# Graph attention layer: smaller halves of work, a ring of 16 tiles and rows that go through memory

## The reference, cut to what matters

```
Wh = x1 @ W;  s_i = Wh @ a1;  s_j = Wh @ a2
e = leaky_relu(s_i[:, :, None] + s_j[:, None, :], 0.2)
e = where(adj > 0 or diagonal, e, -inf)
h = softmax(e, axis=-1) @ Wh
out = layernorm(x1 + elu(h))
```

## Time and profile before

| | us |
|---|---|
| median of 3 runs | 3981.21 |
| lowest, highest | 3978.74, 4451.86 |
| the profiled execution's own time | 3980.02 |
| its span | 3978.2 |

### The profile page before, as it was taken

The page is one execution under the profiler, slowest core; times in us unless marked ns, Lnnn a source line. Parts: engine busy times, 40 slices in busy tenths (PEclk is TensorE's granted clock), DMA queues, the critical chain, the costliest instruction groups (busy, mean ns, idle before and its releaser), DMA issues. The chain is left out here.

```text
span 3978.2 us, 135900 instructions
## 1 busy us (share of the span) xinstructions
PE 3643.7 (92%) x57428; PEld 2511.2 (63%) x57428; DVE 3254.2 (82%) x3989; ACT 2520.5 (63%) x3554; POOL 2064.1 (52%) x1068
## 2 busy tenths in 40 slices
PE   6999999999999999999999999942998998999898
PEld 2656756655756655665665675522776777777777
DVE  6786887787788688688788778857989989889897
ACT  3666666666666666666666666622677676776777
POOL 1786787777678687678677768831101011011010
PEclk9999999999999999999999999976999999999999
DMA  6010010010010001001001000042111110110101
GB/s 216 3 37 16 14 40 14 19 35 19 14 40 14 14 19 40 14 14 40 18 15 35 19 14 19 19 164 78 39 43 33 44 54 24 52 54 22 33 28 37
DMA packets 106692, 145.28 MB, mean 37 GB/s; under 512 B 3792, under 2 KB 87632, under 8 KB 104016
## 3 DMA queue, kind: packets, MB, share of 16 engines
q1 hardware_dynamic: 104816, 135.80, 10.2%
q10 hardware_dynamic: 1248, 0.40, 0.1%
HBM read 102.63 MB, written 33.55 MB: 34 GB/s over the span
## 5 line engine op out<-in xcount | busy, mean ns | idle before, releaser
L277 POOL TENSOR_TENSOR psums<-probs 128x1024 f32<-128x1024 f32 x512 | 1288.8, 2517 | 626.7 <-ACT probs L381 624.4
L381 ACT ACTIVATE probs<-probs 128x1024 f32<-128x1024 f32 x1024 | 1083.5, 1058 | 812.8 <-DVE probs L857 791.2
L493 PE MATMUL ctx_ps<-probs,v_rows 64*32 64x512 f32 x16256 | 1477.1, 590 | 11.7 <-DVE seg_ctx L780 10.3
L857 DVE SCALAR_TENSOR_TENSOR probs<-sc_ps,clip_hi 128x1024 f32<-128x1024 f32 x1024 | 1225.0, 1216 | 217.6 <-PE sc_ps L480 206.6
L480 PE MATMUL sc_ps<-q_cols,k_cols 64*32 64x512 f32 x16384 | 1205.0, 592 | 43.9 <-DVE probs L857 43.3
L1324 PE MATMUL out_ps<-wh,e 128*128 128x257 f32 x4096 | 963.7, 388 | 166.0 <-DVE e L1466 157.2
L1324 PEld LDWEIGHTS out_ps<-wh,e 128*128 128x128 f32 x4096 | 777.5, 193 | 326.6 <-DVE e L1466 117.9
L493 PEld LDWEIGHTS ctx_ps<-probs,v_rows 64*32 64x32 f32 x16256 | 664.0, 106 | 289.9 <-issue 190.6
L480 PEld LDWEIGHTS sc_ps<-q_cols,k_cols 64*32 64x32 f32 x16384 | 533.8, 106 | 333.9 <-issue 212.2
L1153 POOL TENSOR_TENSOR rstd<-var_eps,minus_half 128x4 f32<-128x4 f32 x32 | 68.4, 2138 | 1069.6 <-DVE var_eps L1426 1069.6
L487 PE MATMUL den_ps<-psums,ones 64*32 64x512 f32 x4064 | 598.3, 594 | 17.9 <-DVE seg_ctx L780 11.2
(11 more groups left out here) (97 smaller groups left out, 3356.1 us busy)
## 6 DMA issues: line engine op xcount, KB each, us to landing
x_cols<-in_xT SPq DMA_DIRECT2D x8, 2048.0 KB, 7.9
probs<-in_adjT SPq DMA_DIRECT2D x16, 1024.0 KB, 8.4
x_rows<-in_x SPq DMA_DIRECT2D x32, 512.0 KB, 4.1
x<-res SPq DMA_DIRECT2D x32, 512.0 KB, 2.9
x_in<-x SPq DMA_DIRECT2D x8, 2048.0 KB, 10.3
x_res<-x SPq DMA_DIRECT2D x32, 512.0 KB, 4.7
out<-h SPq DMA_DIRECT2D x32, 512.0 KB, 3.2
e<-in_adjT SPq DMA_DIRECT2D x8, 1024.0 KB, 7.8
```

Of the source, the lines that this page charges most:

```text
L277: pool.tensor_tensor(psums[:, q % 2, pair, :], probs[:, (SJ * q) % RING, pair, :], probs[:, (SJ * q + 1) % RING, pair, :], ALU.add).then_i ...
L381: act.activation(probs[:, n % RING, pair, :], probs[:, n % RING, pair, :], ACT.Exp, scale=DH ** -0.5).then_inc(s_exp, 1)
L493: return pe.matmul(ctx_ps[quad(h), z, :], v_rows[head_rows(r), n % JB, at:at + QUAD], probs[head_rows(r), n % RING, h, :], start=start, st ...
L857: dve.scalar_tensor_tensor(out=probs[:, n % RING, pair, :], in0=sc_ps[:, p, :, :], scalar=-LIM, in1=clip_hi[:, j, c * CW:(c + 1) * CW][:, ...
```

## The change

Only `layer1` changes, save the constant BIG = 2^126.

- Mask: one DVE instruction a piece in place of two; values 0 or -BIG; the diagonal is set to 0. Maxima use add and max, masking is min(mask + BIG, e).
- Maxima by halves of 1024 queries: 32 instructions of 128 x 1024 a batch. Those of half 0 stand at steps 10 to 40 of the batch before, those of half 1 at steps 42 to 72, which is up to step 8 of the batch itself. POOL reduces twice: half 0 at chunk 3 of the batch before, half 1 at chunk 0 of the batch, ahead of that chunk's `inverse_deviation`.
- s_i is a column more of the product with W (258 columns), no longer a row made by PE. SP stores it (2048 values of 4 bytes, `spread_own`) and loads it as 128 x 16; the maxima come as 128 x 8 from partition 0. `row_operations` is four instructions of 128 x 8 for each half (steps 55 and 17). SP stores the result and loads two rows of 1024 queries to all partitions (512 KB each, `make_rows`).
- ERING 16, LRING 8, AHEAD 6, larger side two steps ahead, LATE 5, and EARLY 4: the last 4 steps of a chunk do their right tiles first, with a semaphore `s_right` of their own for `invert`, which waits for the left products before its third reciprocal.
- ELU plus one: `scale_h` adds 1, one ACT pass exp(h - 1), DVE takes max(min(exp, 1), h).
- x1 comes in pieces of 512 KB; the units of preparation are interleaved over steps 1 to 31.
- Moved: invert and scale_h and exp_h to j = 3, residual 8, stats and variance together 9, offset 11, norm_h 12.

```diff
-    ERING = 8
-    AHEAD = 3
-    LRING = 4
+    ERING = 16
+    AHEAD = 6
+    LARGER_AHEAD = 2
+    LRING = 8
-    LATE = 3
+    LATE = 5
+    EARLY = 4
+    INV_AT, ELU_AT, RES_AT, STATS_AT, OFFSET_AT = 3, 6, 8, 9, 11
+    SCALE_AT, EXP_AT, NORM_AT = 3, 3, 12
+    MAX_AT = (10, 42)
+    ROWS_AT = (55, 17)
+    FIFTHS_AT = 45
+    uses_at = [1 + 32 * u // USES for u in range(USES)]
...
+    max_at = {(0, j): MAX_AT[0] + 32 * j // JB for j in range(JB)}
+    max_at.update({(1, j): MAX_AT[1] + 32 * j // JB for j in range(JB)})
...
+            def spread_own(b):
+                sp.wait_ge(s_prepread, count(b, USES, 2 + USES))
+                    sp.dma_start(s_d[0].rearrange("(j p) -> p j", p=P), wh[:, b[1] % 2, :, 0]).then_inc(s_sout, 16)
+                sp.wait_ge(s_sout, count(b, 16, 16))
+                sp.wait_ge(s_rows, count(b, 8))
+                sp.dma_start(s_c[:, :, :], s_d[0].rearrange("(h p j) -> p h j", h=2, p=P)).then_inc(s_sin, 16)
+            def make_rows(b, half, first=False):
+                sp.wait_ge(s_all, count(b, 2, 2 + half + 1))
+                sp.dma_start(m_c[:, :], highest[0:1, :].rearrange("o (q j) -> o q j", j=HJ)).then_inc(s_m, 16)
+                sp.wait_ge(s_rows, count(b, 8, 4 * half + 4))
+                sp.dma_start(rows_d[half].rearrange("r (p j) -> p r j", p=P), rows_c[:, :, :]).then_inc(s_rout, 16)
+                sp.wait_ge(s_rout, count(b, 32, 16 * half + 16))
+                if not first:
+                    sp.wait_ge(s_max, count(b, STEPS, FREE - STEPS + LRING + HSTEPS * (half + 1)))
+                at = slice(half * HW, (half + 1) * HW)
+                sp.dma_start(high[:, at], rows_d[half, 0].partition_broadcast(P)).then_inc(s_rin, 16)
+                sp.dma_start(low[:, at], rows_d[half, 1].partition_broadcast(P)).then_inc(s_rin, 16)
...
+            def reduce(b, half):
+                pool.wait_ge(s_best[half], count(b, JB, JB))
+                pool.wait_ge(s_m, count(b, 32, 16 * half))
+                pool.tensor_tensor(pool_tick[:, :], one[:, :], minus_one[:, :], ALU.add)
+                pool.partition_all_reduce(highest[:, :], best[:, half, :], P, bass.bass_isa.ReduceOp.max)\
                     .then_inc(s_all, 1)
...
             def steps(b, chunks, prev, more):
                 for c in chunks:
+                    if c == 0:
+                        reduce(b, 1)
                     if c == NC - 1 and more:
-                        reduce(following(b))
+                        reduce(following(b), 0)
                     if prev:
                         inverse_deviation(*chunk_before(b, c))
...
-                act.activation(neg[:, :, :], h[:, c % 2, :, :], ACT.Relu, scale=-1.0).then_inc(s_min, 1)
-                act.wait_ge(s_min, count(b, NC, c + 1))
-                act.activation(neg[:, :, :], neg[:, :, :], ACT.Exp, scale=-1.0).then_inc(s_en, 1)
+                act.activation(e_h[:, :, :], h[:, c % 2, :, :], ACT.Exp, bias=minus_one[:, :]).then_inc(s_en, 1)
...
             order = [(j, (0, 1)) for j in range(LATE)] + [(j, (2, 3)) for j in range(LATE)] \
-                + [(j, range(T)) for j in range(LATE, JB)]
+                + [(j, range(T)) for j in range(LATE, JB - EARLY)] \
+                + [(j, (2, 3)) for j in range(JB - EARLY, JB)] + [(j, (0, 1)) for j in range(JB - EARLY, JB)]
...
+            def maximum(b, half, j):
+                    dve.scalar_tensor_tensor(out=own, in0=of, scalar=wh[:, p, j, 1:2], in1=own,
+                                             op0=ALU.add, op1=ALU.max).then_inc(s_best[half], 1)
...
             def invert(b, c):
-                dve.wait_ge(s_mm, count(b, STEPS, ERING + (c + 1) * JB))
+                dve.wait_ge(s_right, count(b, NC, c + 1))
```

More of the change, by code:

```diff
@@ L1078, in layer1 @@
         adj_v = adjT.rearrange("(q a p) (c i) -> c q p a i", p=P, a=4, i=CW)
+        pieces = [(q, c) for h2 in range(2) for q in range(4) for c in (2 * h2, 2 * h2 + 1)]
         block = ctx.enter_context(nc.Block())
@@ L1119, in steps @@
+                    if c == NC - 1 and more:
+                        make_rows(following(b), 0)
                     if not prev:
@@ L1453, in larger_side, with mask_tile @@
                 dve.tensor_tensor(tile, tile, e_low[:, n % LRING, :], ALU.max).then_inc(s_max, 1)
+            def mask_tile(b, n):
+                c, j = divmod(n, JB)
+                tile = e[:, n % ERING, :]
+                dve.wait_ge(s_max, count(b, STEPS, FREE + LRING + n + 1))
+                dve.scalar_tensor_tensor(out=tile, in0=mask[:, j, c * CW:(c + 1) * CW], scalar=BIG,
+                                         in1=tile, op0=ALU.add, op1=ALU.min).then_inc(s_e, 1)
             def steps(b, chunks, prev, more):
@@ L1477, in steps @@
-                        if prev and j == 11:
-                            variance(*before)
-                        if prev and j == 13:
-                            offset(*before)
-                        if more:
-                            for m in range(JB):
-                                if n == max_at(m):
-                                    maximum(following(b), m)
-                            if n == max_at(JB - 1) + 1:
-                                fifths(following(b))
-                            if n in ROWS_AT:
-                                row_operation(following(b), ROWS_AT.index(n))
+                        if prev and j == STATS_AT:
+                            stats(*before)
@@ new lines, in steps @@
+                        if prev and j == OFFSET_AT:
+                            offset(*before)
+                        for due in maxima(b, n, more):
+                            maximum(*due)
+                        if n == FIFTHS_AT and more:
+                            fifths(following(b))
+                        if n == ROWS_AT[1]:
+                            row_operations(b, 1)
+                        if n == ROWS_AT[0] and more:
+                            row_operations(following(b), 0)
@@ L1494, in tail @@
                 residual(b, c)
-                for t in range(T):
-                    stats(b, c, t)
-                variance(b, c)
+                stats(b, c)
                 offset(b, c)
```

375 lines of the change are left out of this document (205 added, 170 removed).

## The result

The changed kernel takes 3939.65 us (median of four runs, 3938.6 to 3940.95) where the kernel before, on the same chip, takes 3980.07: a ratio of 0.99, with a 95% interval of 0.988 to 0.9919. It is faster by 1%, within the 2% of no change, and it missed the 3883 us of the forecast by 57 us, outside the range. One of the four executions of the kernel before took 4451.86 us, far from the other three (3978.74 to 3981.21), and the ratio leaves it out. The profiled execution's own time is 3939.18 us, its span 3937.4.

What follows compares the result with a forecast made beforehand. DVE bounds layer 1's batches, 143.3 of 155.95 us busy, PE near. New batch 134.3 + 4.6 + 4 = 142.9, saving 91 us over 7 batches; start saves 11, last batch loses 7, end saves 2: 3980 to 3883, range 3838 to 3932.

Steps and rivals of the forecast that it cites:

- the wait for POOL: Layer 1, offset at step 11: DVE waits about 4.6 us a batch behind half 1's reduction and inverse_deviation.
- rival 2: POOL changes its code back behind the reduction, another 5.9 us: wait 10.5, batch 148.8, time 3930; chance 0.20.
- Rival 1: The wait at POOL is absorbed and small waits vanish: batch 136.3, time 3834; chance 0.13.
- The start: Layer 1's start up to the first masked tile: 11 us saved, bounds 0 and 20.
- DVE's work: Layer 1's batches: DVE's busy time falls from 143.3 to 134.3 us a batch.
- Depth: Layer 1, ring 16, AHEAD 6, larger side 2 ahead: DVE's other idle time, 12.6 us a batch, becomes 4.
- Rival 3: Depth isn't the cause; the 12.6 us of idle time stay: batch 151.5, time 3943; chance 0.16.
- PE's row units: Layer 1's preparation: PE loses 6.8 us a batch, which brings nothing by itself as DVE stays above it.
- LATE and EARLY at 0: Order of PE's products, covered by its backlog: price 0, or about 1 us a chunk if PE ran dry.
- ACT's pass: ELU: ACT loses a pass a chunk, with four copies 7.0 of 112.7 us a batch, not the bound.
- Transfers hidden: s_i's store lasts 8 us, due 43 later; half 0's row chain takes 13.0 us, covered by DVE's 13.6.
- Rival 4: The store of s_i isn't spread over engines, 127 us: DVE held at step 55, time 4470; chance 0.06.

Runs made afterwards that it cites:

- the first experiment: The changed kernel with inverse_deviation of the chunk before moved ahead of half 1's reduction on POOL: 3860.82 us, ratio 0.9702.
- the shallow kernel: The changed kernel with inverse_deviation ahead of half 1's reduction, and ring 8, AHEAD 3, larger side one ahead, LRING 4: 3881.98 us, ratio 0.9753.

## Why the prediction was wrong

**The step that failed: the wait for POOL, 4.6 us.** It measured 12.4 a batch, because POOL starts late a second time, behind the reduction. The sum had a tick of 0.4, a load of 5.9, a reduction of 3.1 and a power of 1.4 against 6.0 of DVE's work. The trace of the batch shown gives 1.10, 6.43, 3.24, 7.45 and 1.05 against 6.3. The 7.45, 6.7 to 7.2 in the other batches, had no term; it is nearly all of the miss. The text knew of it: it is rival 2, given 0.20, on the ground that the trace of before could not show it. That was the wrong reading of a silence. The row excluded neither case, and what it did show, a gap of 5.86 us each time POOL came from an ordinary operation to a reduction, was a reason for a like price on the way back. Rival 2's own 10.5 was 2 short, the longer tick and gaps. Its time, 3930, is 10 off. Rival 1, that the wait is absorbed, is out: without it a batch is 11.2 us shorter.

**The sum by its terms.** The forecast's batch was 134.3 + 4.6 + 4 = 142.9; it measured 135.7 + 12.4 + 3.3 = 151.4: +1.4, +7.8, -0.7. Over six batches the miss is 6 x 8.5 = 51 us. The start was 3.8 better than said (14.8 in place of 11), and what lies outside the start and the six batches 9 worse, about 8 of it by the wait in the last batch (12.8 where the sum had 4.6). 51 - 3.8 + 9 is the miss of 56 against the profiled execution. With the wait removed, in the first experiment, the batch is 140.25 where the sum without its wait says 138.3.

**DVE's work.** Right to 1%. The half-width maximum was mis-sized: 1.20 us from start to start, not 1.14, 1.8 a batch. The row taken for it reads two tensors of 4 bytes, but the 2-byte mask isn't the reason: 1466 reads it too and lasts 0.68 like 1453. The whole maximum is as much above other operations of its width (2.33 against 2.28), so this looks like a fixed cost of some 0.05 us. Both maxima take a scalar from `wh` for each partition, where the row taken has a constant; whether that is the cause no run shows. The line of the page for it, in the kernel after:

```profile
L1451 DVE SCALAR_TENSOR_TENSOR best<-mask,wh,best 128x1024 f32<-128x1024 bf16 x240 | 319.1, 1330 | 13.4 <-ACT wh L1287 10.2
```

The mean of 1330 ns has some held up in it. One beside half 0's reduction:

```profile
2995.30 2.92 DVE L1451 SCALAR_TENSOR_TENSOR best<-mask,wh,best 128x1024 f32<-128x1024 bf16 x1
```

2.92 in place of 1.28, so 1.6 for a reduction of 3.35 us: the lower bounds for DVE's loss (1.7) and for the reduction (3.06) were the nearer ones. Each of the six has one such instruction of 2.91 or 2.92, also the one reduction among them that lasts 6.68 us in place of 3.35 to 3.61. The four row operations of a half take 0.6 us together, so 1.2 a batch where the sum had 1.0. The instruction began 0.16 us behind the reduction (2995.14) and ended 0.3 ahead of its end. By the rule of the Trainium skill (SBUF — State Buffer, section Who interferes with whom) each of the two locks the other out, and the instruction would have lost the whole of the reduction; the trace shows half, and the measurement decides.

**Depth, 8.6 us.** The total was right, and in part by luck, since the forecast gave it to depth alone. DVE's waits fell from 11.8 to 2.9 a batch, and to 2.7 with the new order. By the runs, in the order in which they took the change apart, of those 9.1: depth 2.7, spreading the maxima 4.3, and 2.1 for the rest. The waits for `neg` (8.0 / 6 = 1.3) and LATE and EARLY (about 1) would fill the rest, but no run shows that they do. The split holds for this order: depth was tried only with the maxima spread, spreading only in the shallow kernel. Rival 3 was right that depth isn't needed for most of it and wrong that the waits stay.

**PE's row units bring nothing:** shown, in the kernel before. **LATE and EARLY at 0:** wrong by about 1 us a batch. **ACT's pass, on an engine that isn't the bound:** under 1 us a batch.

**Transfers hidden:** right in effect. The row chain was costed at 3.2 + 7.8 for store and load; they take 1.6 and 5.3 in the median. ACT still waits for it in four batches of six (25.4 us), but DVE does not wait behind it, and taking the wait away brought nothing. The store of s_i, in pieces of 4 bytes, was said to last 8 us; the load behind it on the same queue, which waits for its end, is issued 10.3 us after it (2822.55, 2832.86). Rival 4 is out.

**PE's clock**, which the forecast left out. Two stretches in and behind the standstill at 3059, and one in the next:

```profile
3060.00:3072.00 12.00, 5.02 (x24) 4.04 (x22) 0.00 (x0) 0.00 (x0) 4.07 (x2) 0.83 0.01 0
3072.00:3080.00 8.00, 4.83 (x17) 3.98 (x18) 7.74 (x12) 7.54 (x15) 0.22 (x1) 0.61 0.01 4
```

```profile
3222.00:3230.00 8.00, 2.79 (x9) 2.42 (x10) 5.70 (x9) 5.50 (x11) 1.05 (x1) 0.50 0.00 0
```

PE's products end at 3065.0, and the next start at 3075.2. The granted clock is 0.83 in the mean of the first stretch, 0.61 in the second and 0.50 in the third, the lower of its two levels (1.2 GHz). In the second DVE is busy 7.74 of 8 us, so PE's slowness doesn't reach it: a loss beside the wait, not on top of it. From 3080 to 3090 the clock is 1.00 again.

## What to carry to other kernels

A gap that an engine shows when it changes its kind of work is to be charged for each way, until a row shows an operation right behind; where an urgent small operation shares POOL with a reduction, the small one goes first, which here was worth about 77 us of 3940 and turned 1% into 3%. Before a wait is put down to a shallow ring, look for steps that carry extra work on the leading engine: spreading that work saved 2.8 us a batch in the shallow kernel, twice the depth 3.1 on top of it. And take the wait off the path and count again what had lain under it: here 1.4 of the 12.4 us came back as busy time.

## What the runs showed that was not expected

POOL stands 6.7 to 7.5 us between a reduction and an ordinary operation, where the way in costs 5.6 to 6.4. Two reductions in a row pay once (5.89, then nothing). In the kernel after, the tick lasts 1.10 us behind 28.9 us of idle time and 0.47 right behind a power; why was not looked into. A store of 2048 pieces of 4 bytes from 128 partitions took about 10 us, no more than the adjacency's pieces of 1 MB there (11.3 in the median, where the forecast had taken the 7.8 of before).
